# Last self attention: scores of four heads issued together, copies shared evenly by ScalarE and VectorE

## The reference

```python
h = _layernorm(x, ln1_g, ln1_b)
x = x + _mha(h, h, sa_wq, sa_bq, sa_wk, sa_bk, sa_wv, sa_bv, sa_wo, sa_bo)
# inside _mha, HEADS=16, HD=16:
scores = jnp.einsum('bhqd,bhkd->bhqk', q, k) * HD ** (-0.5)
p = jax.nn.softmax(scores, axis=-1)
o = jnp.einsum('bhqk,bhkd->bhqd', p, v)
```

## Time and profile before

| | us |
|---|---|
| median of 3 runs | 4755.02 (4749.33 to 4756.09) |
| profiled execution | 4757.91 |
| its span in the trace | 4756.1 |
| PE busy in the span | 3922.0 (82%) |
| DVE busy | 3115.8 (66%) |
| ACT busy | 2330.0 (49%) |
| POOL busy | 2116.6 (45%) |
| mean granted TensorE clock, share of 2.4 GHz | 0.938 |

### The profile page before, as it was taken

One profiled execution on the slowest core, in us unless ns is written; L12 is line 12 of the kernel. 1 busy time (PEld: TensorE's weight loads), 2 busy tenths in 40 slices (PEclk: granted clock), 3 DMA queues, 4 the chain that ended last, 5 costly groups with the idle time before them and its releaser, 6 DMA issues. The chain is left out here.

```text
span 4756.1 us, 51594 instructions
## 1 busy us (share of the span) xinstructions
PE 3922.0 (82%) x16584; PEld 2005.4 (42%) x16584; DVE 3115.8 (66%) x4144; ACT 2330.0 (49%) x4397; POOL 2116.6 (45%) x2146
## 2 busy tenths in 40 slices
PE   6987897798799668888788878887788768889897
PEld 3443343344344324444444444444444434444343
DVE  2543263263335249999899989999899956474553
ACT  2321331232233147776677767776677634343342
POOL 0210020031012047787778867787788833132231
PEclk9998999899899879999999999999999979899999
DMA  3000000000000043222333223222332210000000
GB/s 136 1 1 11 0 1 5 6 1 0 11 1 1 24 116 93 84 67 80 88 87 94 84 80 98 80 67 80 94 95 80 61 57 1 10 1 11 1 6 5
DMA packets 132058, 215.91 MB, mean 45 GB/s; under 512 B 18960, under 2 KB 118544, under 8 KB 124496
## 3 DMA queue, kind: packets, MB, share of 16 engines
q1 hardware_dynamic: 131504, 201.08, 14.7%
q0 software_dynamic: 288, 11.53, 0.6%
HBM read 186.26 MB, written 26.30 MB: 45 GB/s over the span
## 5 line engine op out<-in xcount | busy, mean ns | idle before, releaser
L1612 POOL TENSOR_TENSOR m_db<-m_u,m_bb 128x512 f32<-128x512 f32 (+1 forms) x1280 | 1465.0, 1163 | 456.2 <-DVE m_hh L1564 453.5
L1564 DVE TENSOR_TENSOR_SCAN m_hh<-psum,m_kept,m_db 128x512 f32<-128x512 f32 (+1 forms) x1024 | 1195.0, 1200 | 30.3 <-POOL m_u L1657 17.5
L1363 ACT ACTIVATE psum<-m_dt,m_am 128x512 f32<-128x512 f32 (+1 forms) x1280 | 818.4, 644 | 410.2 <-DVE m_hh L1564 406.5
L1291 PE MATMUL psum<-cst,m_hh 128*128 128x128 f32 x4608 | 665.0, 285 | 325.4 <-DVE m_yt L1578 214.5
L1291 PEld LDWEIGHTS psum<-cst,m_hh 128*128 128x128 f32 x4608 | 525.0, 145 | 761.5 <-DVE m_yt L1578 427.1
L1301 PE MATMUL psum<-m_ys,cst 128*128 128x512 f32 x1024 | 550.5, 620 | 0.0
L651 POOL TENSOR_SCALAR a_pr<-a_pr,a_ri 128x512 f32<-128x512 f32 x256 | 173.9, 692 | 683.9 <-DVE a_ri L593 683.9
L1578 DVE SCALAR_TENSOR_TENSOR m_yt<-psum,m_bc,m_yt 128x512 f32<-128x512 f32 x600 | 436.7, 728 | 55.8 <-PE psum L1291 54.7
L651 POOL TENSOR_SCALAR c_pr<-c_pr,c_ri 128x512 f32<-128x512 f32 x256 | 173.9, 692 | 437.3 <-DVE c_ri L593 437.3
L1375 ACT ACTIVATE m_ys<-psum,m_bc 128x512 f32<-128x512 f32 x512 | 343.9, 672 | 26.5 <-PE psum L1291 25.5
L513 POOL TENSOR_TENSOR a_pr<-a_pr,a_ri 128x512 f32<-128x512 f32 x64 | 66.5, 1042 | 624.8 <-DVE a_ri L481 624.8
(11 more groups left out here) (222 smaller groups left out, 5907.9 us busy)
## 6 DMA issues: line engine op xcount, KB each, us to landing
m_bb<-b_rows SPq DMA_DIRECT2D x48, 1024.0 KB, 4.7
m_xr<-x_line SPq DMA_DIRECT2D x128, 192.0 KB, 3.6
m_bb<-b_rows SPq DMA_DIRECT2D x32, 768.0 KB, 4.3
m_xr<-x_line SPq DMA_DIRECT2D x128, 160.0 KB, 3.4
m_xr<-x_line SPq DMA_DIRECT2D x128, 128.0 KB, 3.0
m_xr<-x_line SPq DMA_DIRECT2D x128, 96.0 KB, 3.1
a_w1b<-w1b_in POOLq DMA_DIRECT2D x1, 7168.0 KB, 29.2
x_line<-m_xc SPq DMA_DIRECT2D x32, 192.0 KB, 4.4
```

What stands on the lines that cost most here:

```text
L1291: mm = nc.tensor.transpose(s[:, e * P:(e + 1) * P], hh[:, n % 2, e, t * P:(t + 1) * P], ident)
L1363: nc.scalar.activation(bank(DECAY[u % len(DECAY)])[:, 0:w], dt[:, g % 2, e, 0:w], ACT.Exp, scale=am[:, layer_of(g) % 2, e * DS + n:e * DS ...
L1564: nc.vector.tensor_tensor_scan(hh[:, n % 2, e, 0:w], bank(DECAY[u % len(DECAY)])[:, 0:w], db[:, u % 4, 0:w], kept[:, n, e:e + 1] if g % NI ...
L1612: nc.gpsimd.tensor_tensor(db[:, u % 4, 0:w], us[:, g % 2, e, 0:w], bb[:, at % 2, n % 4, 0:w], ALU.mult).then_inc(pool_done, pr.pool.step(f ...
```

## The change

The last self attention gets functions of its own, `pe_quads`, `dve_quads` and `act_quads`, and a plan `QuadPlan`; the other self attention keeps the old ones. The arithmetic of a unit is the same. What differs is the grouping and the order:

- PE issues the scores of four units at once: four heads on four row groups, the same query tile, into all four score banks, with one semaphore step for the four. It waits for the exponentials of the four units before.
- The units of a block are counted by query tile first, and the flips follow one step behind the scores (four flips a step) where they were two steps behind.
- The copies go to ACT for even units and to DVE for odd ones, which with the two flip banks ties each bank to one engine.
- The weighing is issued after the flips of every second step.

The stage has 16 steps of four units in place of 32 of two.

```diff
+class QuadPlan:
+    def unit(self, u):
+        heads, half, _, _ = self.blocks[u // 8]
+        return heads[u % 4], 2 * half + u // 4 % 2
+    def by_act(self, u):
+        return u % 2 == 0
...
+            def pe_quads(self, pe, name, q, k_of, v_of, plan):
+                def scores(i):
+                    units = range(4 * i, 4 * i + 4)
+                    found = [self.scr.take(f"{name} s {u}", p.act, f"{name} exp {u}") for u in units]
+                    for _, emptied in found:
+                        if emptied:
+                            pe.wait_ge(*emptied)
+                    for u, (b, _) in zip(units, found):
+                        h, qt = plan.unit(u)
+                        rows, tile, keys = k_of(h)
+                        mm = nc.tensor.matmul(b, q[rows, tile, qt * P:(qt + 1) * P], keys, start=True, stop=True)
+                    mm.then_inc(pe_done, p.pe.step(f"{name} s {i}"))
...
+                for i in range(plan.n + 2):
+                    if i < plan.n:
+                        scores(i)
+                    if 1 <= i <= plan.n:
+                        for u in range(4 * i - 4, 4 * i):
+                            flip(u)
+                    if i >= 3 and i % 2 == 1:
+                        weigh((i - 3) // 2)
...
+            def dve_quads(self, dve, name, plan, dst, bias):
+                for i in range(plan.n + 2):
+                    if i >= 1 and i <= plan.n:
+                        inverse(2 * i - 1)
+                    if i < plan.n:
+                        maximum(2 * i)
+                        maximum(2 * i + 1)
+                    if 1 <= i <= plan.n:
+                        empty(4 * i - 3)
+                    if i < plan.n:
+                        inverse(2 * i)
+                    if 1 <= i <= plan.n:
+                        empty(4 * i - 1)
...
+            def act_quads(self, act, name, plan):
+                for i in range(plan.n + 1):
+                    if i >= 1:
+                        empty(4 * i - 4)
+                    if i < plan.n:
+                        for u in range(4 * i, 4 * i + 4):
+                            act.wait_ge(dve_done, p.dve.at(f"{name} max {u // 2}"))
...
+                    if i >= 1:
+                        empty(4 * i - 2)
...
-            plan3 = SelfPlan([(tuple(8 * g + odd + 2 * i for i in range(4)), half, g, (half, odd) == (0, 0))
-                              for g in range(2) for half in range(2) for odd in range(2)], 4)
+            plan3 = QuadPlan([(tuple(8 * g + odd + 2 * i for i in range(4)), half, g, (half, odd) == (0, 0))
+                              for g in range(2) for half in range(2) for odd in range(2)])
...
-                            st.pe_self(pe, f"{a} s3", q3, keys_of, values_of, plan3)
+                            st.pe_quads(pe, f"{a} s3", q3, keys_of, values_of, plan3)
```

More of the change, by code:

```diff
@@ L645, in act_self, with flip, weigh @@
                                                      ACT.Copy).then_inc(act_done, p.act.step(f"{name} flipped {u}"))
-            def pool_self(self, pool, name, plan):
+            def pe_quads(self, pe, name, q, k_of, v_of, plan):
                 p = self.prog
-                for u in range(2 * plan.n):
+                banks = {}
+                def scores(i):
[9 more added lines that the diff above has]
+                    mm.then_inc(pe_done, p.pe.step(f"{name} s {i}"))
+                def flip(u):
+                    b, emptied = self.trn.take(f"{name} t {u}", p.act if plan.by_act(u) else p.dve, f"{name} flipped {u}")
+                    if emptied:
+                        pe.wait_ge(*emptied)
+                    pe.wait_ge(pool_done, p.pool.at(f"{name} normed {u}"))
+                    for kt in range(NT):
+                        mm = nc.tensor.transpose(b[:, kt * P:(kt + 1) * P], self.pr[:, u % 6, kt * P:(kt + 1) * P],
+                                                 ident)
+                    mm.then_inc(pe_done, p.pe.step(f"{name} t {u}"))
+                def weigh(k):
+                    heads, half, g, opens = plan.blocks[k]
+                    if opens:
+                        banks[g], emptied = self.lin.take(f"{name} o {g}", p.dve, f"{name} o {g} out")
+                        if emptied:
+                            pe.wait_ge(*emptied)
+                    pe.wait_ge(dve_done, p.dve.at(f"{name} flipped {8 * k + 7}"))
+                    pe.wait_ge(act_done, p.act.at(f"{name} flipped {8 * k + 6}"))
+                    for kt in range(NT):
+                        for n, h in enumerate(heads):
+                            values, rows, first, last = v_of(h, kt)
+                            mm = nc.tensor.matmul(banks[g][rows, half * 2 * P:(half + 1) * 2 * P], values,
+                                                  self.ptr[k % 2][:, n, kt, :], start=first, stop=last)
+                    mm.then_inc(pe_done, p.pe.step(f"{name} w {k}"))
+                for i in range(plan.n + 2):
[6 more added lines that the diff above has]
+                        weigh((i - 3) // 2)
@@ new lines, in dve_quads, with maximum, inverse, empty @@
+            def dve_quads(self, dve, name, plan, dst, bias):
+                p = self.prog
+                def maximum(j):
+                    u = 2 * j
+                    dve.wait_ge(pe_done, p.pe.at(f"{name} s {j // 2}"))
+                    if j >= 4:
+                        dve.wait_ge(act_done, p.act.at(f"{name} exp {u - 7}"))
+                    b = p.bank_of(f"{name} s {u}")
+                    nc.vector.tensor_reduce(self.nm[:, u % 8:u % 8 + 2],
+                                            psum[:, b * BANK:(b + 2) * BANK].rearrange("p (u t) -> p u t", u=2),
+                                            AX.X, ALU.max, negate=True)\
+                        .then_inc(dve_done, p.dve.step(f"{name} max {j}"))
+                def inverse(j):
+                    u = 2 * j
+                    dve.wait_ge(act_done, p.act.at(f"{name} exp {u + 1}"))
+                    if j >= 4:
+                        dve.wait_ge(pool_done, p.pool.at(f"{name} normed {u - 7}"))
+                    nc.vector.reciprocal(self.rih[:, u % 8:u % 8 + 2], self.smh[:, u % 8:u % 8 + 2])\
+                        .then_inc(dve_done, p.dve.step(f"{name} inverse {j}"))
+                def empty(u):
+                    dve.wait_ge(pe_done, p.pe.at(f"{name} t {u}"))
+                    if u >= 16:
+                        dve.wait_ge(pe_done, p.pe.at(f"{name} w {u // 8 - 2}"))
+                    nc.vector.tensor_copy(plan.flipped(self.ptr, u),
+                                          self.full(f"{name} t {u}").rearrange("p (k t) -> p k t", k=NT))\
+                        .then_inc(dve_done, p.dve.step(f"{name} flipped {u}"))
+                def output(g):
+                    dve.wait_ge(pe_done, p.pe.at(f"{name} w {plan.closing[g]}"))
+                    nc.vector.tensor_scalar(dst[:, g, :], self.full(f"{name} o {g}"), bias[:, g:g + 1], None,
+                                            ALU.add).then_inc(dve_done, p.dve.step(f"{name} o {g} out"))
+                for i in range(plan.n + 2):
[10 more added lines that the diff above has]
+                        empty(4 * i - 1)
+                    if i >= 4 and i % 2 == 0 and (i - 4) // 2 in plan.closing.values():
+                        output(plan.blocks[(i - 4) // 2][2])
+                output(plan.blocks[-1][2])
@@ L650, in pool_self @@
+            def pool_self(self, pool, name, units):
+                p = self.prog
+                for u in range(units):
                     pool.wait_ge(dve_done, p.dve.at(f"{name} inverse {u // 2}"))
@@ L2027, in _ @@
                         if a is not None:
-                            st.pool_self(pool, f"{a} s3", plan3)
+                            st.pool_self(pool, f"{a} s3", 4 * plan3.n)
             found["c"] = pr.result()
```

27 lines of the change are left out of this document (24 added, 3 removed).

## The result

The changed kernel takes 4740.26 us, the median of 7 runs (4731.34 to 4750.5), against 4752.85 us for the kernel before in its 7 (4749.33 to 4760.1). The ratio is 0.9971, with a 95% interval of 0.9959 to 0.9982: 0.29% faster, and 1 lies outside the interval. The profiled execution took 4740.26 us, its span is 4738.5 us.

A forecast was written before the change was run, and what follows sets the result against it. Bound by a chain through every engine, PE close to its limit, and second by the clock. Stage: fill 24.4, six blocks of 12.0, drain 5.1, output 0.8, clock 2.5: 104.8 us, -7.6 for four, forecast 4748, range 4733 to 4776.

The forecast's parts named there:

- rival 1: The clock holds after the fill: four stages of 102.3 us, -17.6 us, 4737 in all; chance 0.24.
- The steps: Steady part: a step without a weighing takes 5.39 us, one with a weighing 6.62 us.
- the block: Two steps, 8 units, in the steady part: 12.0 us against 11.88 before; +0.8 us over six blocks.
- The group of four: Scores of four heads on four row groups overlap fully: 1.15 us to the end, 1.06 us of PE.
- The drain: Stage end, weighing before last to the last: 5.1 us in place of 9.1, -4.0 a stage, trusted most.
- ScalarE's copies: Steady part: four ACT copies a block, 0.59 us each, lie beside the maxima and cost nothing.
- Rival 3: The four heads don't overlap fully: 4767 with a group of 1.45 us, 4802 with pairs in turn; chance 0.12.
- The 1.38 us: PE time of a group of four scores by the skill's 3.07 times: 20 us more, to about 4768.
- The fill: Stage start, first scores to end of weighing 0: 24.4 us against 25.9, -1.5, bounds -3.0 and +2.1.
- four heads keep all four row groups at work: In the fill, reason for expecting only one or two slow steps at 1.2 GHz, a step about 6.7 us.
- clock falls in the steady part: One or two of seven blocks disturbed at 1.7 us each: +2.5 us a stage, bounds 0 and +11.9.
- Rival 2: The clock falls in every block: +11.9 us a stage, 4785 at worst, 4768 with five or six; chance 0.16.

The follow-up runs named there:

- experiment 1: Changed kernel with each group of four scores made of two heads at two query tiles, so only two row groups are used: 4794.96 us, ratio 1.0098.
- experiment 3: Changed kernel with the weighing put between the second and third flip of its step: 4705.04 us, ratio 0.9901.
- experiment 4: Changed kernel with four more full matmuls, result unused, behind the first scores of every stage: 4728.23 us, ratio 0.9956.
- 7: Kernel of experiment 3 with the weighing cut in two halves, one in each step: 4699.40 us, ratio 0.9880.
- 6: Kernel of experiment 3 with each group of four scores split into two pairs that wait and report on their own: 4688.65 us, ratio 0.9857.
- experiment 5: Changed kernel with copies shared as before, three of four by VectorE and one by ScalarE: 4794.75 us, ratio 1.0080.
- experiment 8: Kernel of experiment 3 with both pairs that wait on their own and the weighing in two halves: 4689.97 us, ratio 0.9859.
- experiment 2: Kernel before with every second copy by ScalarE in place of every fourth, nothing else: 4751.48 us, ratio 0.9999.

## Why the prediction was right, and where it was not

The time was forecast at 4748 and came at 4740.3, inside the range and by the mechanism that was named. The number lies nearer to the 4737 of rival 1, but rival 1 isn't what happened: the clock fell 15 times behind the fill. Of the 7.7 us between forecast and result, 0.6 are rounding, 2.2 are the kernel before, whose median is 4752.85 over seven runs where three had given 4755.0, 3.9 are the stages (11.5 gained where 7.6 were forecast, on the profiled executions), and 1.1 remain.

**Confirmed, to a tenth.** The steps: 5.40 and 6.65 us where 5.39 and 6.62 were worked out, the block 12.05 against 12.0. The group of four: 1.14 to its end against 1.15. The drain: 5.18 against 5.1. Each is what the sum was built from, and experiments 1 and 3 move them by what the same chain gives (+0.83 a group; 6.65 back to 5.39). ScalarE's copies lie beside the maxima: PE waits 0.25 us for one and then 1.15 for DVE's, which ends later.

Which part of the change brought the shorter drain, by which it gains most, is read from the timelines and from the order of the instructions: flips one step behind in place of two. No run keeps pairs of scores and moves only the flips, so whether the drain could be had without the groups of four isn't shown.

**Rival 3 is out.** The group holds PE for 1.07 us, as a pair did (1.06), and the stages would be 58 us longer without overlap by experiment 1, where I had put 55. The 1.38 us that I had worked out with a page's figure took 1.06 us for each of four matmuls, but 0.2 us of that come only once in a row of them: the four full ones of experiment 4 take 3.70 us, not 4.24, so four heads on four row groups, at 1.14 us, are 3.25 times as fast. The Trainium skill's 3.07 times ("TensorE: Matmul & The Clock Gate", "Part 3: Packing small matmuls — row/col tiling") would make 3.70 us into 1.21, an estimate; the 1.14 measured here is a little better and not far from it.

**The fill: right size, wrong reason.** As a mean, weighing 0 ends at 23.9 us where 24.4 was put. In stage 1 one step runs at 1.2 GHz for the most part, 6.6 us (3912.68 to 3919.26) where about 6.7 was put, and I had taken one or two. I had argued that four heads keep all four row groups at work and that this brings the clock back. Experiment 1 has it back before the weighing on two row groups too, though 3.4 us later, and experiment 4 shows that avoiding the first fall only moves it to 12 to 17 us. What in the new order of the fill brings the clock back after 6.9 us and not 20.5 is open.

**The mis-sized term: clock falls in the steady part.** I took one or two blocks of seven at 1.7 us each, +2.5 a stage. There are 3.75 falls a stage, and the 24 blocks (six a stage) took 6.7 us more than 24 x 12.05, 0.45 a fall: +1.7 a stage. The price was worked out as if a fall lasted through a block. It lasts 3.4 us, and PE waits for other engines in a part of it anyway. The number of falls was put too low and the price of one too high; that the two nearly cancel is luck. Rival 2 was mis-sized with it: at 0.45 us a fall in each of seven blocks would be about 3 us a stage and not 11.9 (an estimate from this kernel's falls). Its 4768 for five or six blocks was also added up wrongly: on my own price it is 4771 to 4778. The falls behind the first of each stage are 15 in the changed kernel, 9 in experiment 3, one in 7 and none in 6, where PE's waits are shorter one after the other, and 32 in experiment 5, where they are longer; why one comes in one block and not in the next is open.

**Not foreseen: 5.1 us outside the stages.** The prediction counted nothing there. The four stretches behind the stages hold the same instructions in all kernels and took 415.7 to 421.4 us. The stretch behind stage 1, in the changed kernel and in the kernel before:

```profile
4010.80:4114.60 103.80, 86.78 (x224) 39.82 (x224) 43.74 (x78) 28.04 (x50) 8.32 (x8) 0.93 0.00 0
```

```profile
4015.60:4121.70 106.10, 89.08 (x224) 40.54 (x224) 43.82 (x77) 28.04 (x50) 8.32 (x8) 0.92 0.00 0
```

PE is busy 2.3 us longer in the second at the same 224 matmuls, DVE and ACT are not: the time is the clock's (13.7 us at 1.2 GHz against 17.1). It is the same in the other profiles: of the first three stretches those with 13.7 us low took 103.8 to 104.7 us and those with 17.1 took 105.6 to 106.2 (and the one with 10.2, in experiment 8, 103.0). It isn't a property of the change: experiment 2, whose stages are like those of before, has 416.8 in these stretches, and experiment 3 has 421.4. The profiled execution of the kernel before is also 5.1 us above the median of its runs, and that of the changed kernel is its median: between the medians lie 12.6 us, which leaves about 1 us beside the stages. By that the change itself is worth the 11.5 us of the stages, and the forecast for them was 7.6.

## What to carry to other kernels

Where several engines form a chain, halving the work of one of them returns only what the chain allows: here 2.1 us of PE work a block were gained and the block became 0.17 us longer. Experiments 3 and 6 say what held it: 1.27 us the weighing that stood in order behind a waiting flip (12.05 to 10.78), and 0.45 the four banks that were filled, and so emptied, at once (10.78 to 10.33). What gained was the shorter drain. So look at what stands in order behind a waiting instruction: moving the weighing ahead of the flip that waits (31.4 us) and giving each pair its own wait (22.7 us) were each worth more than the change itself.

## What the runs showed of the hardware

- Four matmuls of 32 rows on four row groups take as long as two on two: 1.14 against 1.13 us for 512 columns in float32. On two row groups four of them take 1.99, and four full ones one after another (128 rows, experiment 4) 3.70.
- TensorE's clock falls for 3.4 us at a time in a pattern whose waits are 0.25, 1.15 and 0.52 us, and such a fall costs 0.45 us on average of 15, where PE waits for other engines anyway. In the old fill it stayed low for 17.1 to 23.9 us, and in stage 1 PE was busy for all of its 20.5 us.
- The same instructions ahead of stage 1 took 3897.4 to 3908.4 us in these profiles, at granted clocks of 0.95 and 0.94. Here are the first and the last of them, experiment 4 and the kernel before:

```profile
0.00:3897.40 3897.40, 3188.78 (x13184) 1647.76 (x13185) 2659.08 (x3400) 2000.24 (x3628) 1912.14 (x1858) 0.95 0.19 54
```

```profile
0.00:3908.40 3908.40, 3206.05 (x13184) 1657.74 (x13185) 2659.72 (x3400) 1998.88 (x3628) 1909.41 (x1858) 0.94 0.19 54
```

PE is busy 17.3 us longer in the second, while DVE, ACT and POOL differ by less than 3 us. Between two profiles of this kernel, 10 us are therefore no evidence for a change unless the stage that changed shows them.
